# A chunked gated delta-rule scan: its Gram products spread over the hops, a second output Gram tile, and unused identity products in TensorE's gaps

## What is computed

```python
q, k, v = silu(causal_conv4(x @ W.T) + bias) per stream;  k *= 128 ** -0.5
a = sigmoid(x @ Wa.T + ba);  beta = sigmoid(x @ Wb.T + bb)
def step(St, inp):                      # per head: St is 128 x 128
    kt, qt, vt, at, bt = inp
    Sk = einsum('bhij,bhj->bhi', St, kt)
    err = Sk - vt
    Sn = at[..., None] * St - (bt[..., None] * err)[..., None] * kt[:, :, None, :]
    ot = einsum('bhij,bhj->bhi', Sn, qt)
    return (Sn, ot)
_, outs = scan(step, S0, ...)           # 2048 tokens, 16 heads
x = x + (layernorm(outs) * ln_g + ln_b) * sigmoid(x @ Wg.T) @ Wo.T
x = x + ffn(layernorm(x));  x = x + heavy_hitter_attention(layernorm(x));  x = x + ffn(layernorm(x))
```

## Time and profile before

| | us |
|---|---|
| median of three runs | 8566.85 |
| profiled execution | 8577.77 |
| its span | 8576.0 |
| TensorE busy | 6556.2 (76%) |
| VectorE busy | 4972.7 (58%) |
| ScalarE busy | 2404.3 (28%) |
| scan, first state product to last solve | 1139 to 3843 |

### The profile page before, as it was taken

One profiled execution on the slowest core, in us unless ns is written; L12 is line 12 of the kernel. 1 busy time (PEld: TensorE's weight loads), 2 busy tenths in 40 slices (PEclk: granted clock), 3 DMA queues, 4 the chain that ended last, 5 costly groups with the idle time before them and its releaser, 6 DMA issues. The chain is left out here.

```text
span 8576.0 us, 84049 instructions
## 1 busy us (share of the span) xinstructions
PE 6556.2 (76%) x26502; PEld 4452.5 (52%) x26502; DVE 4972.7 (58%) x8482; ACT 2404.3 (28%) x4766; POOL 736.0 (9%) x360
## 2 busy tenths in 40 slices
PE   2888857777777777767979959645429889998899
PEld 1666645555555555554547844322218722222587
DVE  2888856666666666665663222687887733333322
ACT  1222222222222222224432111344412133333111
POOL 0555500000000000001101101000000000000011
PEclk6999956666666666668989979656655588887899
DMA  4333332322222122212120031111102221111200
GB/s 153 119 137 133 133 90 55 84 55 55 62 77 59 54 62 79 55 34 101 47 71 30 22 113 74 55 30 32 27 18 60 50 45 30 30 39 43 82 26 27
DMA packets 554973, 545.85 MB, mean 64 GB/s; under 512 B 69072, under 2 KB 473296, under 8 KB 529616
## 3 DMA queue, kind: packets, MB, share of 16 engines
q1 hardware_dynamic: 554624, 541.59, 21.4%
HBM read 380.16 MB, written 161.35 MB: 63 GB/s over the span
## 5 line engine op out<-in xcount | busy, mean ns | idle before, releaser
L297 PE MATMUL proj_acc<-proj_xn,proj_w 128*128 128x512 f32 x3072 | 728.4, 400 | 126.3 <-ACT proj_decay L343 91.1
L2313 PE MATMUL attend_ot<-attend_e,attend_v 128*64 128x512 f32 (+3 forms) x1280 | 687.7, 628 | 91.4 <-ACT attend_e L2340 91.4
L297 PEld LDWEIGHTS proj_acc<-proj_xn,proj_w 128*128 128x128 f32 x3072 | 594.0, 194 | 260.8 <-ACT proj_decay L343 94.1
L1937 PE MATMUL csum_sc<-csum_qk 96*128 96x512 f32 (+3 forms) x640 | 289.2, 568 | 395.6 <-ACT csum_e L1961 349.9
L390 DVE SCALAR_TENSOR_TENSOR proj_y<-proj_raw,proj_cw,proj_y 128x2048 f32<-128x2048 f32 x144 | 575.5, 3996 | 19.1 <-DVE proj_y L386 3.0
L1610 DVE TENSOR_TENSOR scan_part<-scan_y_ps,scan_before 128x64 f32<-128x64 f32 x512 | 114.6, 224 | 792.5 <-PE scan_y_ps L1305 494.4
L1370 ACT ACTIVATE scan_zt<-scan_zt_ps 64x128 f32<-64x128 f32 (+2 forms) x448 | 129.1, 288 | 1490.7 <-PE scan_zt_ps L1255 1050.7
L1305 PE MATMUL scan_y_ps<-scan_ring,scan_ST 128*128 128x64 f32 x2048 | 449.8, 420 | 66.3 <-ACT scan_ST L1370 42.8
L1305 PEld LDWEIGHTS scan_y_ps<-scan_ring,scan_ST 128*128 128x128 f32 x2048 | 438.5, 330 | 84.4 <-ACT scan_ST L1370 43.5
L885 POOL TENSOR_TENSOR ffn_hid_low<-ffn_hid,ffn_hid_high 128x512 fp32r<-128x512 f32 x128 | 164.6, 1286 | 3574.5 <-ACT ffn_hid_high L875 3574.5
L938 DVE TENSOR_TENSOR ffn_hid<-ffn_gate,ffn_l 128x512 f32<-128x512 f32 x128 | 88.0, 688 | 582.7 <-PE ffn_l L821 351.8
(11 more groups left out here) (260 smaller groups left out, 13467.6 us busy)
## 6 DMA issues: line engine op xcount, KB each, us to landing
scan_abar<-decays SPq DMA_DIRECT2D x256, 256.0 KB, 4.2
csum_qk<-qk SPq DMA_DIRECT2D x96, 256.0 KB
cmax_qk<-qk SPq DMA_DIRECT2D x96, 256.0 KB
attend_qk<-qk SPq DMA_DIRECT2D x96, 256.0 KB
proj_beta_rows<-beta SPq DMA_DIRECT2D x16, 1024.0 KB, 8.1
stream_k<-proj_res SPq DMA_DIRECT2D x16, 1024.0 KB, 3.9
stream_beta_k<-proj_resb SPq DMA_DIRECT2D x16, 1024.0 KB, 3.9
stream_beta_v<-proj_resb SPq DMA_DIRECT2D x16, 1024.0 KB, 3.8
```

Of the source, the lines that this page charges most:

```text
L297: mm = pe.matmul(acc[:, (j * TT + t) % 8, :], w[:, u, wh, j, k, :], xn[:, xh, k, t * TOK:(t + 1) * TOK], start=(p == 0 and k == 0), stop=( ...
L1937: pe.matmul(sc[:, n % 2, c:c + w], qk[:, u, 0, q * P:(q + 1) * P], qk[:, u, 1, c:c + w], start=True, stop=(c + w < (q + 1) * P))
L2313: pe.matmul(ot[:, g % 2, lo:TOK], v[:, u, kt, :], e[:, x % RINGS, lo:TOK], start=(kt == 0), stop=(x == last_of[g])).then_inc(summed, 1)
```

## The change

- `go21` and `go0`, the masked output Gram tiles in SBUF, get two buffers, by the block's parity `p`.
- The Gram products of the next block (`gram2`, `gram3`) move ahead of hop 0; `gram_out0` goes behind hop 0 and `gram_out21` behind hop 1 (they stood behind hops 5 and 4); `turn_u`, `turn_v`, `k_rows` and `spread_far` each move one place later or so.
- The copies `k4` and `k8` get a semaphore of their own (`kblk_copied`) and are made two blocks ahead, as is `stage_keys`.
- VectorE's `mask23`, `mask_out0`, `mask_out21` and the state decays of banks 3 and 2 move to behind solves 0 to 3, `far` and `far3` one solve later, the state decay of bank 0 to behind solve 6 and that of bank 1 to behind solve 7. The wait for `abar` goes with the first of them, to behind solve 2.
- `stay(n)` is new: n float32 products of the identity with a 128x256 constant into `zt_ps`, which nobody reads. They stand behind `gram_out0` (1), before hops 4 and 5 (2 each), behind hop 6 (4) and at the end of the body (3).
- On ScalarE the copies follow: `keys(..., 3)` of the next block stands behind `near`, `near` itself stays between hops 4 and 5.

```diff
         g4 = sb("g4", [P, 2, 2, 8, 32])
-        go21 = sb("go21", [P, 2, 2, P])
-        go0 = sb("go0", [P, 4, P])
+        go21 = sb("go21", [P, 2, 2, 2, P])
+        go0 = sb("go0", [P, 2, 4, P])
         zt = sb("zt", [P, 2, P])
         ztf = sb("ztf", [P, 4, P])
         ut = sb("ut", [P, 4, P])
         kt_copied = sem("kt_copied")
...
                 loaded(it, u)
-                pe.wait_ge(kin_copied, 4 * (it * BPR + u) + 2)
+                pe.wait_ge(kblk_copied, 2 * (it * BPR + u) + 1)
                 for j in range(4):
...
-                    mm = pe.matmul(o, vt[:, 2 + g, :], go21[:, 0, g, :], start=False, stop=True, skip_group_check=True)
+                    mm = pe.matmul(o, vt[:, 2 + g, :], go21[:, p, 0, g, :], start=False, stop=True, skip_group_check=True)
...
-                    pe.matmul(yo_ps[:, 8 * g:8 * g + 8, 1::2], vt[:, g, :], go21[:, 1, g, :], start=False, stop=True, skip_group_check=True)
+                    pe.matmul(yo_ps[:, 8 * g:8 * g + 8, 1::2], vt[:, g, :], go21[:, p, 1, g, :], start=False, stop=True, skip_group_check=True)
                 for g in range(4):
-                    mm = pe.matmul(yo_ps[:, 4 * g:4 * g + 4, :], ut[:, g, :], go0[:, g, :], start=False, stop=True, skip_group_check=True)
+                    mm = pe.matmul(yo_ps[:, 4 * g:4 * g + 4, :], ut[:, g, :], go0[:, p, g, :], start=False, stop=True, skip_group_check=True)
+
+            def stay(n):
+
+                for _ in range(n):
+                    pe.matmul(zt_ps[:, 0:2, :].rearrange("p a b -> p (a b)"), idt[:, :], om[:, :, :].rearrange("p a b -> p (a b)"), start=True, stop=True)
@@ -1305,43 +1311,46 @@
                 mm.then_inc(pq_done, 1)
-                if not first:
-                    turn_u(b - 1, (u + 1) % 2)
+                if left:
+                    pe.wait_ge(gch_masked, 2 * b + 2)
+                    gram2(ni, nu)
+                    gram3(ni, nu)
                 pe.wait_ge(gch_masked, 2 * b + 1)
                 hop(b, u, 0)
                 if not first:
-                    turn_v(b - 1)
-                    pe.wait_ge(ut_copied, 2 * b - 1)
-                if left:
-                    k_rows(ni, nu)
+                    turn_u(b - 1, (u + 1) % 2)
+                gram_out0(u)
+                stay(1)
                 hop(b, u, 1)
                 if left:
-                    pe.wait_ge(gch_masked, 2 * b + 1)
-                    gram2(ni, nu)
+                    pe.wait_ge(gch_masked, 2 * b + 3)
+                gram_out21(b, u)
+                if not first:
+                    turn_v(b - 1)
+                hop(b, u, 2)
+                if left:
                     if not first:
                         pe.wait_ge(ut_copied, 2 * b)
+                    k_rows(ni, nu)
                     spread_far(ni, nu)
-                hop(b, u, 2)
-                if left:
-                    gram3(ni, nu)
                 if not first:
-                    out_pairs(b - 1)
+                    out_pairs(b - 1, (u + 1) % 2)
                 pe.wait_ge(gch_masked, 2 * b + 2)
                 hop(b, u, 3)
                 if left:
                     pe.wait_ge(kt_copied, b + 2)
                     spread_near(ni, nu)
+                stay(2)
                 hop(b, u, 4)
                 if left:
                     pe.wait_ge(inv_step, 8 * (b + 1) + 1)
                     gram4(ni, nu)
-                    pe.wait_ge(gch_masked, 2 * b + 3)
-                gram_out21(b, u)
+                stay(2)
                 hop(b, u, 5)
-                gram_out0(u)
                 if not first:
-                    out_ones(b - 1)
+                    out_ones(b - 1, (u + 1) % 2)
                 hop(b, u, 6)
+                stay(4)
...
                 mm.then_inc(ds_done, 1)
+                stay(3)
...
@@ -1380,20 +1390,21 @@
                 if k == 0:
                     act.wait_ge(chunk_in[u // BPS], 80 * (it + 1))
                     if not (isinstance(c, int) and c < 2):
-                        act.wait_ge(go_done, 2 * c - 2)
+                        act.wait_ge(go_done, 2 * c - 3)
                     copy(kall[:, u % 2], x).then_inc(kin_copied, 1)
                 elif k == 1:
+                    act.wait_ge(chunk_in[u // BPS], 80 * (it + 1))
                     if not first:
                         act.wait_ge(gch_done, 2 * c - 1)
-                    copy(k4[:, :, :, :], x.rearrange("p h (j t) -> p j h t", t=8)[:, :, :, 0:4]).then_inc(kin_copied, 1)
-                    copy(k8[:, :, :, :], x.rearrange("p h (j t) -> p j h t", t=16)[:, :, :, 0:8]).then_inc(kin_copied, 1)
+                    copy(k4[:, :, :, :], x.rearrange("p h (j t) -> p j h t", t=8)[:, :, :, 0:4]).then_inc(kblk_copied, 1)
+                    copy(k8[:, :, :, :], x.rearrange("p h (j t) -> p j h t", t=16)[:, :, :, 0:8]).then_inc(kblk_copied, 1)
                 elif k == 2:
                     if not first:
                         act.wait_ge(gch_done, 2 * c)
                     copy(k16[:, :, :], x[:, :, 0:16]).then_inc(kin_copied, 1)
                 else:
                     if not first:
-                        act.wait_ge(go_done, 2 * c - 1)
+                        act.wait_ge(go_done, 2 * c)
                     copy(kpair[:, :, :, :], blocks(KK, u)[:, :, :, 0:2])
                     copy(keven[:, :, :], x[:, :, 0::2]).then_inc(kout_copied, 1)
 
@@ -1446,8 +1457,11 @@
 
             def prologue():
                 act.wait_ge(init, NINIT)
-                for k in range(3):
-                    keys(0, 0, k)
+                keys(0, 0, 1)
+                keys(0, 0, 0)
+                keys(0, 0, 2)
+                keys(0, 0, 3)
+                keys(0, 1, 1)
                 k_rows(0, 0)
                 tables(0, 0)
                 near(0, 0)
@@ -1457,24 +1471,25 @@
                 first = isinstance(b, int) and b == 0
                 ni, nu = next_of(it, u, 1)
                 hop(b, u, 0)
+                if left:
+                    keys(ni, nu, 0)
+                hop(b, u, 1)
                 if not first:
                     turned(b - 1, 0)
-                if left:
-                    keys(ni, nu, 0)
-                    keys(ni, nu, 1)
-                hop(b, u, 1)
+                if left > 1:
+                    keys(*next_of(it, u, 2), 1)
+                hop(b, u, 2)
                 if not first:
                     turned(b - 1, 1)
                 if left:
-                    k_rows(b + 1, nu % 2)
-                hop(b, u, 2)
-                if left:
                     keys(ni, nu, 2)
                 hop(b, u, 3)
-                keys(it, u, 3)
...
@@ -1581,16 +1596,16 @@
                 dve.tensor_tensor(g4[:, p], w_ps[:, QG4].rearrange("p a b -> p (a b)").rearrange("p (g h x) -> p g h x", g=2, h=8),
                                   bm[:, 2].unsqueeze(1).unsqueeze(3).to_broadcast([P, 2, 8, 32]), mult).then_inc(gch_masked, 1)
 
-            def mask_out21(c):
+            def mask_out21(c, p):
+                dve.wait_ge(go_done, 2 * c + 2)
+                dve.tensor_tensor(go21[:, p], w_ps[:, Q23].rearrange("p (l g) x -> p l g x", l=2),
+                                  om[:, :, :].unsqueeze(2).to_broadcast([P, 2, 2, P]), mult).then_inc(go_masked, 1)
+
+            def mask_out0(c, p):
                 dve.wait_ge(go_done, 2 * c + 1)
-                if not (isinstance(c, int) and c < 1):
-                    dve.wait_ge(xo_done, 2 * c)
-                dve.tensor_tensor(go21[:, :, :, :], w_ps[:, Q23].rearrange("p (l g) x -> p l g x", l=2),
-                                  om[:, :, :].unsqueeze(2).to_broadcast([P, 2, 2, P]), mult).then_inc(go_masked, 1)
-
-            def mask_out0(c):
-                dve.wait_ge(go_done, 2 * c + 2)
-                dve.tensor_tensor(go0[:, :, :], w_ps[:, QG0], om[:, 1].unsqueeze(1).to_broadcast([P, 4, P]), mult).then_inc(go_masked, 1)
+                if not (isinstance(c, int) and c < 2):
+                    dve.wait_ge(xo_done, 2 * c - 2)
+                dve.tensor_tensor(go0[:, p], w_ps[:, QG0], om[:, 1].unsqueeze(1).to_broadcast([P, 4, P]), mult).then_inc(go_masked, 1)
 
             def decay_state(b, q):
...
@@ -1665,55 +1681,53 @@
                 dve.wait_ge(tab_copied, b + 1)
                 solve(b, u, 0)
                 decay_y(b, u, 0)
+                decay_z(Z8[:, :, 0:4], Z4[:, :, :], z0 + 1, tot4[:, p, :, 1:2])
                 if left:
-                    stage_keys(ni, nu)
-                decay_z(Z8[:, :, 0:4], Z4[:, :, :], z0 + 1, tot4[:, p, :, 1:2])
+                    skip_decay(b + 1, nu)
+                    mask23(b + 1, np_)
                 solve(b, u, 1)
                 decay_y(b, u, 1)
-                if left:
-                    skip_decay(b + 1, nu)
+                mask_out0(b, p)
                 solve(b, u, 2)
                 decay_y(b, u, 2)
                 decay_z(Z16[:, :, 8:12], Z4[:, :, :], z0 + 4, tot4[:, p, :, 3:4])
```

(61 more changed lines are left out.)

2 lines of the change are left out of this document (1 added, 1 removed).

## The result

The changed kernel takes 8282.98 us, median of four runs (8269.99 to 8289.02), beside 8565.92 for the kernel before; the ratio is 0.9666, 95% interval 0.9649 to 0.9683, so 283 us are gone. The forecast was 8385, with a range of 8230 to 8520: direction and range held, the size was short by 102 us (181 forecast, 283 measured). The profiled execution took 8283.94.

The account below looks back on a forecast made before the run. The prediction took a chain of solves and hops, with TensorE's clock low for half of each block, as the bound. Gains of 480 us less 160 for clock falls and 140 for late matrices gave 180, so 8385 us, range 8230 to 8520.

Parts of the forecast that it names:

- (a): Block end: state product 7.09 to 3.68, transposes faster, end products costing 0.5, small matmuls unchanged; 3.4 us a block gained.
- (b): Hops 0, 1 and 2: 1.83 to 1.33 us each at the full clock; 1.5 us a block gained.
- (c): Hop 3, four times the columns: 3.60 to 2.3 us at the full clock; 1.3 us a block gained.
- (d): Hop 6: three VectorE passes leave the gap and one comes in; 1.3 us a block gained.
- (e): Hops 4 and 5: nothing gained; between 0.9 us better and 0.5 worse, taken as 0.
- the hold: On ScalarE after solve 5, `near` waits for the moved `far3` ahead of hop 5's copy; 2.9 us instead of 3.06.
- (f): TensorE clock falls at hop 5 and the block end in some blocks: 2.5 us a block, 160 us lost.
- (g): Decay matrices late for the wait moved behind solve 2: VectorE waits 9.1 us, 14 times; 140 us lost.
- held: Rival: the clock never falls for long, only the late decay matrices cost; 8237 us, chance 0.20.
- Falls: Rival: clock falls at hop 5 or block end, returns only by hop 3; about 8530 us, chance 0.15.
- abar in time: Rival: the decay matrices arrive in time, needing a transfer a third faster; 8247 us, chance 0.06.
- Slower: Rival: clock low through whole blocks, inserted work in the way; 9190 us if all blocks, chance 0.07.

Follow-up runs that it names:

- both_no_end: Changed kernel with decay matrices issued first, `far3` ahead of solve 5, and the three unused products at the block's end removed: 8134.60 us, ratio 0.9478.
- no_stay: Changed kernel without its unused products, order and second tile kept: 8560.08 us, ratio 0.9986 to the kernel before.
- far3_early: Changed kernel with `far3` moved back from behind solve 5 to behind `far`: 8213.69 us, ratio 0.9576 to the kernel before.
- abar_first: Changed kernel with SP issuing the decay matrices' loads ahead of the ring's loads and the store: 8104.13 us, ratio 0.9449 to the kernel before.
- old_order_stay: Kernel before with only the unused products added, in its old order: 8528.48 us, ratio 0.9950.
- both_ahead0: Changed kernel, decay matrices issued first, `far3` ahead of solve 5, two unused products ahead of hop 0 replacing the one behind `gram_out0`: 8026.32 us, ratio 0.9365.

## Why the prediction was right, and where it was off

The signs that were named all came: state product 3.68, hops 0 to 2 at 1.30 to 1.36, mean clock 0.90, `part` of solve 7 2.2 behind z, and 14 waits of 9.3 on average. One sign of being wrong came too, in 26 blocks: TensorE late to z with an unused product in front of it.

**(a) Block end**, 3.4: measured 4.17 (13.69 to 9.52). The state product is 3.68 as said. The term is short by what I left unchanged: the 32 small matmuls take 1.17, not 2.09. The Trainium skill ("TensorE: Matmul & The Clock Gate", section "Wait — 56ns, not 53.3ns?") gives about 62 ns for each MATMUL with hardware decode off. The row's 65 ns at the low clock seemed to agree, but at the full clock the same 32 records take 37 ns each, or 73 for each of the 16 products that they stand for. Counted by records the figure would hold them at 1.98, which they beat; counted by products at 0.99, which they don't reach; either way the term was not 0. Which decode was on no run shows. A row at one clock can't tell an issue limit from an array limit. The three end products cost about the assumed 0.5 (`both_no_end`, median).

**(b)** 1.5: measured 1.51 in the medians. **(c)** 1.3: 1.39. **(d)** 1.3: 1.23. **(d)** stands on VectorE's passes and not on the clock, and `no_stay` has most of it (6-7 at 4.20). **(e)** 0: 0.08 and 0.02 worse, and by the hold that was named: `far3_early` takes 0.88 out of the gap. So the clean block was forecast 7.5 shorter and is 8.20: 480 should have been 517.

**(f) Clock falls**, 160: this is the term that was mis-sized. In `abar_first`, which has no wait for the matrices, the mean block is 1.40 over its medians, 88 us, of which 26 were there before (42.26 less 41.84): 62 us. About 28 of them lie at the loop's turns and in the blocks behind them, 23 in other late hops 1, the rest mostly in long 7-next. The place was only half right too. The fall at hop 5, where TensorE idles longest, is there, in 20 blocks of the changed kernel and at 1.6 each, where I worked out 2.2; `far3_early` shows that the hold brings it. But the more frequent one, in 26 blocks, comes at the block's start, behind narrow products and a shorter gap, and costs 1.6 because slower Gram products and an unused one then stand in the way. I also missed the loop's turn: there TensorE waits 2.98 us for no row's event ("issue"), and the state product runs low in 7.09:

```profile
2976.98 7.09 PE L1311 MATMUL scan_y_ps<-scan_ring,scan_ST 128*128 128x64 f32 x32 [2.98 <-issue]
```

**(g) The decay matrices**, 140: 14 waits, of 9.3 on average against 9.1 worked out. With the falls that they bring the experiment gives 186, since what follows costs more than the 2 I gave it, and nothing of it came back as I had assumed.

By the profiles: 517 held, less 62 for falls, less 180 for the matrices, is 275, against the 276 of the means. The forecast had 480, 160 and 140. So the mechanism is the one forecast, each term has the right sign, and the miss is the 98 of the falls and the 37 of the clean block, of which the matrices' 40 took part back. The range's upper end, 8520, lay under the 8530 of the rival that it is named for; nothing hung on it.

The rival *held* was wrong: the clock does fall. *Falls* was wrong in the changed kernel, but `no_stay` and `old_order_stay` are that case, at 8560 and 8528. The Trainium skill's rule on transposes (same page, "Part 4: PE-mode transpose") stays open; no run here separated it. *abar in time* is what `abar_first` makes true. *Slower* did not come: in all 20 blocks in which the unused products behind hop 6 ran low, the small matmuls behind them were back at 1.17.

## What to carry to other kernels

Work that only keeps TensorE's clock up paid here where the gaps it had to bridge were short (347 us, in the old order 43). So first order the other engines so that no gap outlasts it, then place it where the engine idles ahead of the next step, not behind work that may already be late. When a wait is moved forward, count the transfer from its issue: an order on the DMA queue that was free before can cost as much as the move brings, and changing it here was worth 186 us. Judge such a change by the distances between steps over all blocks, medians beside means; the difference names the stalls that one block's timeline doesn't show. And look whether the block on show is an ordinary one: behind a turn of the loop it is not.

## What the runs showed that was not expected

- The row-split matmuls (32 rows, 128 columns) go with the clock: 2.09 to 1.17 us for 32 records.
- The granted clock fell from 0.97 to 0.50 behind the narrow Gram products, with no gap before hop 0 over 1.1 us. With two wide products there (`both_ahead0`) hop 1 is late in 2 blocks instead of 40.
- One stall brings the next: late matrices in 2-3 were followed by the clock's fall at hop 5 of the same block in 11 of 14 blocks, and in none once `far3` was moved (`far3_early`), though the matrices were nearly as late (122.2 us in 14 waits).
- The loop's turn costs more at the full clock than before: blocks 23, 31, 39 of the changed kernel take 40.3 to 40.6 us beside 33.6, before 45.5 to 45.7 beside 41.8.
